# Layer 1 of a two-layer graph network: one node table in place of two, with repeated rows merged over 512 edges

## The reference

```python
edge_index = jnp.stack([src, dst])
deg = jnp.maximum(segment_sum(ones, dst, 100000), 1.0)
deg_isqrt = deg ** (-0.5)
h = jnp.maximum(_layernorm(x), 0.0)
# layer 0: scaled rows h[dst] * edge_weight, summed into the row src
x = x + deg_isqrt * segment_sum((deg_isqrt * h)[dst] * edge_weight[:, None], src)
h = jnp.maximum(_layernorm(x), 0.0)
# layer 1: an MLP (512 -> 512 -> 256) for each edge, averaged over each dst
feat = jnp.concatenate([h[dst], h[src] - h[dst]], axis=-1)
msg = jax.nn.relu(feat @ W1 + b1) @ W2 + b2
x = x + segment_sum(msg, dst) / (segment_sum(ones, dst) + 1e-8)
```

## Time and profile before

| | us |
|---|---|
| median of 3 runs | 2267.06 |
| lowest and highest | 2262.39, 2270.36 |
| profiled execution, its own time | 2282.08 |
| its span, first to last instruction | 2280.2 |

### The profile page before, as it was taken

How to read it: one execution, slowest core, us unless ns; L and a number is a source line. 1 busy time by engine, 2 the same in 40 slices (tenths; PEclk the granted TensorE clock), 3 DMA queues, 4 the chain that set the end, 5 groups by cost and what they waited for, 6 DMA issues and landing times.

```text
span 2280.2 us, 46975 instructions
## 1 busy us (share of the span) xinstructions
PE 1762.0 (77%) x14020; PEld 1536.3 (67%) x14020; DVE 1500.0 (66%) x6001; ACT 1033.7 (45%) x2106; POOL 1280.2 (56%) x1024
## 2 busy tenths in 40 slices
PE   7958888776665667207888888999999999999960
PEld 2258778776665657206777777788888888888850
DVE  8979888886666667205555555667777777777730
ACT  0025454443333333105544554566666666666630
POOL 2032222478888888653332222248888888888754
PEclk9989899998888778658998888999999999999985
DMA  8999999466666666458999999225555555555533
GB/s 297 316 297 338 310 338 311 116 109 101 104 103 104 103 103 104 56 140 279 309 299 295 297 295 292 64 65 94 91 95 97 93 96 99 94 92 97 88 44 39
DMA packets 142793, 379.71 MB, mean 167 GB/s; under 512 B 31805, under 2 KB 97352, under 8 KB 129864
## 3 DMA queue, kind: packets, MB, share of 16 engines
q0 software_dynamic: 86400, 131.14, 32.5%
q1 hardware_dynamic: 27452, 208.63, 26.6%
q10 hardware_dynamic: 28912, 39.64, 6.7%
HBM read 325.72 MB, written 259.17 MB: 257 GB/s over the span
## 4 chain that ended last, share of the span: by engine, by line
PE 24%; issue 11%; POOL 10%; ACT 5%; DMA 3%; DVE 2%; another core or an unknown queue 1%; ACTq 0%; DVEq 0%; POOLq 0%
PE ps_h L1213 12%; PE ps_m L1227 7%; POOL table_out L919 5%; POOL ends L907 5%; PE ps_t L1200 2%; ACT e_normed L1111 2%; DMA table_out<-e_ring,e_targets_all 2%; PE ps_s L1240 2%; ACT hid L1125 1%; DMA ends<-x,keys 1%; DVE e_moments L960 1%; ACT feat_hi L1118 1%; ACT e_ring L1143 0%; DVE out_sum L1032 0%
## 5 line engine op out<-in xcount | busy, mean ns | idle before, releaser
L907 POOL DMA_INDIRECT ends<-x,keys x400 | 402.1, 1005 | 437.4 <-ACT e_normed L1111 312.9
L768 PE MATMUL ps_deg<-table,hot 128*128 128x128 bf16 x5600 | 358.1, 225 | 82.9 <-issue 69.4
L768 PEld LDWEIGHTS ps_deg<-table,hot 128*128 128x128 bf16 x5600 | 334.5, 101 | 101.8 <-issue 92.2
L919 POOL DMA_INDIRECT table_out<-e_ring,e_targets_all x200 | 326.6, 1633 | 108.0 <-issue 54.8
L461 POOL DMA_INDIRECT x<-sums_ring,targets_all x200 | 329.6, 1648 | 89.3 <-issue 65.8
L451 POOL DMA_INDIRECT rows<-in_x,row_idx x200 | 207.4, 1037 | 252.2 <-ACT normed L695 198.2
L1213 PE MATMUL ps_h<-feat_hi,w_hi 128*128 128x512 f32 x800 | 321.3, 402 | 8.9 <-ACT hid L1125 6.5
L1213 PE MATMUL ps_h<-feat_lo,w_hi 128*128 128x512 f32 x800 | 318.8, 399 | 0.5 <-issue 0.5
L1213 PE MATMUL ps_h<-feat_hi,w_lo 128*128 128x512 f32 x800 | 318.2, 398 | 0.7 <-issue 0.7
L782 PE MATMUL ps_sum<-msg_hi,same 128*128 128x260 f32 x800 | 153.3, 321 | 158.8 <-issue 151.7
L1227 PE MATMUL ps_m<-w_hi,hid_hi 128*128 128x256 f32 x800 | 243.1, 304 | 15.6 <-issue 8.3
(11 more groups left out here) (140 smaller groups left out, 3593.6 us busy)
## 6 DMA issues: line engine op xcount, KB each, us to landing
table_out<-x SPq DMA_DIRECT2D x400, 252.0 KB
x<-in_x SPq DMA_DIRECT2D x400, 250.0 KB
hi_row<-hi_rows ACTq DMA_DIRECT2D x50, 256.0 KB
src_row<-src_rows ACTq DMA_DIRECT2D x50, 256.0 KB
dst_row<-dst_rows ACTq DMA_DIRECT2D x50, 256.0 KB
ends<-x,keys POOLq DMA_INDIRECT x400
rows<-in_x,row_idx POOLq DMA_INDIRECT x200
x<-sums_ring,targets_all POOLq DMA_INDIRECT x200
```

Source lines behind the costliest of these rows:

```text
L768: last = nc.tensor.matmul(ps_deg[q][k][:, j * P:(j + 1) * P], hot[:, c, k, j * P:(j + 1) * P], table[:, c, part, :], start=(c == 0 and par ...
L907: pool.indirect_dma_start(out=ends[b % 2][:, n, :], out_offset=None, in_=x1_d, in_offset=bass.IndirectOffsetOnAxis(ap=keys[:, 1 - end, at: ...
L919: pool.indirect_dma_start(out=out, out_offset=bass.IndirectOffsetOnAxis(ap=e_targets_all[:, b, j:j + 1], axis=0), in_=e_ring[:, b % RING1, ...
```

## The change

There is one table, `out`. The copy of `x` goes straight to it, layer 0 adds into it, layer 1 gathers from it and adds into it. So every gather of layer 1 has to be done before its first scatter.

- GpSimd gathers all 50 batches first, one behind the other. The first two go to `ends`, the others to two staging buffers, `stage_rows`. SyncE stores each half of a staging buffer to memory (`ends_d`), and GpSimd waits for that store before it gathers into the half again.
- ScalarE loads the batch after next from `ends_d` into `ends` at the start of each step (`load_ends`, two DMAs of 512 KB). The normalised rows are written over the gathered ones; `e_normed` is gone.
- ScalarE scales the sums into one of two buffers, `e_sums`, and stores them to memory (`keep`, one DMA of 512 KB a batch). The ring of 20 batches is gone.
- When the gathers are over, SyncE loads the sums back into the staging buffers (BACK = 4 batches at a time), and GpSimd scatters them.
- Repeated rows are merged over DW = 4 tiles, the whole batch: `peers` and `peers_after` are 128 x 512 for each tile, the sums take 32 matmuls a batch, and GpSimd waits once after four scatters.
- Tensors that only layer 0 needs are given back before layer 1 begins.

```diff
@@ layer 0 @@
-                            out=x1_d, out_offset=bass.IndirectOffsetOnAxis(ap=targets_all[:, b, j:j + 1], axis=0),
+                            out=out, out_offset=bass.IndirectOffsetOnAxis(ap=targets_all[:, b, j:j + 1], axis=0),
@@ layer 1, sync @@
-                for k in range(FLIGHT):
-                    sp.dma_start(out_flat[k], x1_flat[k]).then_inc(bulk_out[k], 16)
-                with sp.Fori(1, ROUNDS) as r:
-                    ...
+                with sp.Fori(0, HALF - 1) as t:
+                    for q in range(2):
+                        for end in range(2):
+                            sp.wait_ge(staged[q][end], 16 * W * (t + 1))
+                            sp.dma_start(ends_d[bass.ds(2 * t + 2 + q, 1), :, end * W * D:(end + 1) * W * D]
+                                         .rearrange("o p w -> (o p) w"),
+                                         stage_rows[q][:, end * W:(end + 1) * W, :].rearrange("p j d -> p (j d)"))\
+                                .then_inc(spilled[q][end], 16)
+                for q in range(2):
+                    for end in range(2):
+                        sp.wait_ge(spilled[q][end], 16 * (HALF - 1))
+                for b in range(NB):
+                    sp.wait_ge(kept[b % 2], 16 * (b // 2 + 1))
+                    if b >= BACK:
+                        sp.wait_ge(back_free, b - BACK + 1)
+                    sp.dma_start(back(b).rearrange("p j d -> p (j d)"), sums_d[b, :, :]).then_inc(back_in[b % BACK], 16)
@@ layer 1, gpsimd @@
-                    if n == 0 and b >= 2:
-                        pool.wait_ge(e_normed_done, b + 1)
+                    if b >= 4 and j == 0:
+                        pool.wait_ge(spilled[b % 2][end], 16 * (b // 2 - 1))
...
-                for b in range(LEAD1):
+                for b in range(NB):
                     for n in range(2 * W):
                         gather(b, n)
-                for k in range(FLIGHT):
-                    pool.wait_ge(bulk_out[k], 16 * ROUNDS)
-                left = 2 * W * (NB - LEAD1)
-                for c in range(GROUPS * NB):
-                    scatter(c // GROUPS, c % GROUPS)
-                    for n in range(min(left, 3 * c), min(left, 3 * (c + 1))):
-                        gather(LEAD1 + n // (2 * W), n % (2 * W))
-                    scatter_end(c // GROUPS, c % GROUPS)
+                for q in range(2):
+                    pool.wait_ge(ends_first[q], 16 * 2 * W)
+                    for end in range(2):
+                        pool.wait_ge(spilled[q][end], 16 * (HALF - 1))
+                for b in range(NB):
+                    for g in range(GROUPS):
+                        scatter(b, g)
+                        scatter_end(b, g)
@@ layer 1, vector @@
-                        last = nc.vector.tensor_scalar(peers[q][:, j, :], dst_row[q][:, g * G * P:(g + 1) * G * P],
+                        last = nc.vector.tensor_scalar(peers[q][:, j, :], dst_row[q][:, w * DW * P:(w + 1) * DW * P],
@@ layer 1, scalar @@
+                def load_ends(b, t, q):
+                    act.wait_ge(turned, KF * (b - 1))
+                    for end in range(2):
+                        act.wait_ge(spilled[q][end], 16 * t)
+                        act.dma_start(ends[q][:, end * W:(end + 1) * W, :].rearrange("p j d -> p (j d)"),
+                                      ends_d[bass.ds(b, 1), :, end * W * D:(end + 1) * W * D]
+                                      .rearrange("o p w -> (o p) w")).then_inc(ends_in[q], 16)
+                def keep(b, q):
+                    act.wait_ge(e_scaled, GROUPS * (b + 2))
+                    act.dma_start(sums_d[bass.ds(b, 1), :, :].rearrange("o p w -> (o p) w"),
+                                  e_sums[q][:].rearrange("p j d -> p (j d)")).then_inc(kept[q], 16)
@@ layer 1, tensor @@
-                        pe.wait_ge(out_lo_done, GROUPS * b + g + 1)
+                        if g * G % DW == 0:
+                            pe.wait_ge(out_lo_done, GROUPS * b + g + DW // G)
...
-                                for j in range(G * g, G * g + G):
+                                for j in range(w, w + DW):
```

172 lines of the change are left out of this document (97 added, 75 removed).

## The result

The changed kernel takes 2687.6 us (median of 4 runs, 2683.0 to 2692.2) where the kernel before takes 2268.7 beside it (4 runs, 2262.4 to 2279.9): a ratio of 1.184, interval 1.179 to 1.189. It is 18% slower. The forecast was 2,220 and the range ended at 2,410.

The account below looks back on a forecast made before the run. TensorE was taken to bound layer 1's steps, GpSimd's scatters its end. First matmul run at 1,033, plus 49 x 23.5, 28, 3 + 3 + 11 + 3.6: span 2,233, time 2,235, less 15: 2,220; range 2,200 to 2,410.

Parts of the forecast that it names:

- The copy goes: Layer 1: without the copy into out, 15 steps gain 6.9 us each, 100 us, and the end no longer waits for it.
- The sums double: TensorE in layer 1: 32 matmuls at ps_s instead of 16, 1.9 us more in each of 50 steps, 94 us.
- the 0.65 us that the sum added on top: Layer 1's step: what the present 21.1 us has over 20.45, a step almost without waits, added to the forecast step.
- Wider masks on VectorE: Layer 1: masks of 512 columns cost VectorE 0.5 to 2.4 us a step; taken at nothing, uncovered up to 0.5 us.
- More issues on ScalarE and the loads: ScalarE in layer 1: two loads and one store more, 0.34 us each; 0 to 1.0 us a step, taken at 0.5.
- The gathers come first: GpSimd, layer 1: 400 gathers back to back, 1.25 us each, 500 us in all, over at about 1,510; spills taken as fitting.
- rival A: Layer 1: successive gathers hold up compute engines, 3.5 us for each 10 us of gathers; 2,398; chance 0.32, shared with another rival.
- Traffic: Layer 1: spill, reload, store and reload of sums; DMA share about 0.9 during the gathers, cost taken at nothing.
- Scatters last: GpSimd, layer 1: four scatters with one wait take 10.2 us, 50 batches 510 us, following the computation without arrears at the end.
- End: After the last scaling: 3 us out, 3 back, 11 for four scatters and landing, 3.6 to the end of the span.
- Rivals B and C: Layer 1: late reloads or handoffs, 2,270 to 2,320, chance 0.14; GpSimd setting the end again, 2,325 at 16 us, chance 0.10.

Follow-up runs that it names:

- experiment 7: Kernel before, with 392 of the 400 pieces of the copy of x1 to out left out; 2185.2 us, one run, beside 2267.9.
- experiments 4 and 8: First: changed kernel merging over two tiles, 2281.5 us beside 2151.8. Second: kernel before merging over four tiles, ring of 19, 2316.5 us beside 2267.9.
- experiment 5: The changed kernel itself, unaltered, run again on a chip of the first kind; 2214.2 us against 2160.3, ratio 1.024.
- 15: Changed kernel with loads reading x and six stretches of gathers, differently spaced or waited for, the last without stores; second kind, 2571.1 us beside 2269.6.
- 16: Changed kernel with a memset of 128x300 behind every gather of layer 1, second kind; 2343.1 us, ratio 1.027.
- 18: Kernel before, last 11 batches merged over four tiles, 128x300 memset behind layer 1's first 160 gathers, ring of 18; second kind, 2215.9 us, ratio 0.973.
- four of mine: Changed kernel without stores of staged rows, with a wait every fourth gather, with 128x800 memsets, or merging over two tiles: 2209.2, 2393.4, 2382.1, 2281.5 us.

## Why the prediction was wrong, point by point

1. *The copy goes.* Right: 100 us forecast, 83 measured in experiment 7, with 5 of the 7 us a step due to it. It is so on the second kind alone: on the first the steps beside the copy are as short as any.
2. *The sums double.* Right in kind, mis-sized: 1.3 us a step in experiments 4 and 8, for 1.9. TensorE's 16 more matmuls do take their time (32 in 3.8 us in experiment 5, for 1.89 before); but the step of before had waits (the 0.65 us that the sum added on top), and a part of them now lies under the longer sums. That last is argued, not shown.
3. *Wider masks on VectorE.* They take 482 and 747 ns for 373 and 482 before, 1.5 us a step, inside the 0.5 to 2.4. What they cost the step is inside the 1.3.
4. *More issues on ScalarE and the loads.* Taken at 0.5 us a step. On the first kind all that is neither the merge nor the stores costs 0.9 together; how much of it is issues, no run shows.
5. *The gathers come first.* The step that failed. What it says of GpSimd is right: the last gather is issued at 1528, and of GpSimd's waits before gathers all 120.8 us are "issue", so the spill fits. But the sum has 49 steps of 23.5 us from 1,033 on, so it puts what the gathers do to TensorE at nothing; that was set aside as rival A. Measured, TensorE gets rid of one instruction in 1.40 us beside them, and 488 us are lost.
6. *Traffic.* Right, cheaper still: a share of 0.65 to 0.86, and the stores cost 0.1 us a step.
7. *Scatters last.* Right: 10.25 us a batch for 10.2 when they come without a pause, and in the changed kernel no arrears.
8. *End.* 21 us from last scaling to the end of the span, 24 measured (2656.7 to 2681.1).

The sum gave steps of 23.5 us, and in the open they take 22.65. So where no gathers run the forecast is good to 4%. On the first kind the changed kernel takes 2214, which the 2,220 seems to meet; but the kernel before takes 2155 there, and the forecast meant 2,220 against 2,267. Had all this been measured on the first kind, it would have missed the sign all the same, because there the copy costs nothing that could be won.

*Rival A* named the mechanism, its place, and the sign in the trace (gaps in TensorE under "issue" inside groups, and quick steps behind the last gather: both are there). It mis-sized it. The price was 3.5 us lost for 10 us of gathers, read from bursts of eight. Measured in the stream: 488 us lost in some 530 us of gathers, 9.2 for 10. The row that was set against it, eight statistics in 2.71 us, is one of VectorE, and VectorE is not slowed in the stall either (four `peers` in 1.87 us from 1069.36, 1.85 in experiment 5); only a row of TensorE could have spoken against A. Experiment 7 prices a burst at 2 us. The burst was the wrong thing to scale. The pauses begin only late in it, as its own rows show once one looks: in the kernel before, the group that makes VectorE wait 5.77 us has its first pause at 1450.78, 7.9 us after the burst began at 1442.90:

```profile
1450.78 0.28 PE L1227 MATMUL ps_m<-w_hi,hid_lo 128*128 128x256 f32 x1 [0.22 <-issue]
1451.50 0.28 PE L1227 MATMUL ps_m<-w_hi,hid_hi 128*128 128x256 f32 x1 [0.43 <-issue]
...
1452.21 0.28 PE L1227 MATMUL ps_m<-w_hi,hid_hi 128*128 128x256 f32 x1 [0.20 <-issue]
1453.62 0.28 PE L1227 MATMUL ps_m<-w_lo,hid_hi 128*128 128x256 f32 x1 [1.13 <-issue]
```

Four pauses in the last two microseconds of the burst and after it, none in its first seven: a price that grows with the length of the run. The bursts under the copy say the same. From the one at 1106.1 to the one at 1412.3, 47 to 52 matmuls start in the first 7 us of each, and 4 to 7 in the next 5; on the first kind, with the same code, 60 and 29 to 31. Divided by the whole burst it looks like 3.5 for 10. For what follows when the run doesn't end, the rate in its last part had to be taken: 1452.21 to 1453.62 are 1.41 us for one matmul and its load, which otherwise take 0.12 here. From this row alone 500 us of gathers would have been priced at some 460 us lost (an estimate: 500 x (1 - 0.12 / 1.41)), against 488 measured. The range of 2,410 was the end of an average, not of the unknown.

*Rivals B and C* did not come: from 1600 on VectorE does not stand before its statistics at all (0.0 us in 45 steps), and no gather waits for a spill.

## What to carry to other kernels

A cost read from a short burst must not be multiplied by the length of a long one: look in the burst's rows for when it begins, and price what lies beyond with its last part. A queue of GpSimd's indirect gathers without a pause can stop TensorE on some chips, while the profile shows DMA engines half idle and nothing that TensorE waits for. Leaving 2 us from one to the next, or waiting for a landing every four (2 us on average as well), took the stall away in one trace (15), and 0.36 us more between them took away 345 us in 16 and 48 in 18. It is worth trying where GpSimd has time. Whether a kernel that isn't being recorded has the stall at all is open (next section). And where a change's result can't be understood, run both kernels once more, on another chip, before taking any experiment's word: four of mine seemed to cure a stall that wasn't there.

## What the runs showed of the hardware

- Two kinds of chip, by what TensorE does beside GpSimd's indirect gathers. Second kind: one instruction in 1.40 us with gathers 1.25 us apart, 14 to 48 matmuls in 10 us at 1.5 us, full speed (60) at 2 us. First kind: full speed at all three. They differ too in the copy's rate, 342 and 297 GB/s. That the engines meet only at semaphores, as the description of the chip above has it, does not hold on the second kind.
```profile
1110.86 0.35 POOL L970 MEMSET filler<- 128x300 f32 x1 [1.34 <-remote]
1111.37 0.95 POOL L940 DMA_INDIRECT stage_rows<-table_out,keys  x1 [0.15 <-issue]
1112.97 0.35 POOL L970 MEMSET filler<- 128x300 f32 x1 [0.65 <-remote]
```

  In the changed kernel its last gathers, from 1513 on, come 1.40 us apart in place of 1.25. The pauses come in about 0.7 and 1.4 us on both engines, which points to something shared; what it is no run tells, and it stays open.
- The DMA engines are not busy: their share is 0.37 in the stretch in which TensorE is slowest. The Trainium skill ("SBUF — State Buffer", SBUF: two separate sides) says that a DMA can't be slowed by a compute operation nor the reverse, and that TensorE never waits on another engine for its ports. On the first kind the trace agrees (62 matmuls in 10 us). On the second kind TensorE falls to 4 in 10 us beside the same stream, so the sentence can't be relied on beside these DMAs. Whether SBUF's ports have a part in it, or the path lies elsewhere, no run here shows.
